# Two quads of attention heads share 32 PSUM rows, and are copied out, turned back and divided per pair

## The chip, the cores and the metric

The kernel runs on one core of one Trainium2 chip. The metric is the device time of one execution in microseconds (us); lower is better. Engines: PE is TensorE (matrix products and transposes; PEld are its weight loads), DVE is VectorE, ACT is ScalarE, POOL is GpSimd, SP only issues DMAs here.

## The reference

Eight sublayers are applied in turn to x (16 batches of 128 tokens, 128 features), each as x = x + tanh(gate) * f(layernorm(x)). The context is 16 x 128 x 128. Cut to what matters:

```
x += tanh(g_xattn[0]) * L0_xattn(ln(x), ctx)    # 0: linear causal attention
x += tanh(g_ffn[0])   * L0_ffn(ln(x))           # 1: 8 experts
x += tanh(g_xattn[1]) * L1_xattn(ln(x), ctx)    # 2: one-head attention
x += tanh(g_ffn[1])   * L1_ffn(ln(x))           # 3: 16 experts and a shared one
x += tanh(g_xattn[2]) * L2_xattn(ln(x), ctx, ctx, mask)  # 4: 16 heads of width 8
x += tanh(g_ffn[2])   * L2_ffn(ln(x))           # 5: 64 slots with a GRU step
x += tanh(g_xattn[3]) * L3_xattn(ln(x), ctx, ctx)        # 6: 16 heads; 8 of them on every 2nd token
x += tanh(g_ffn[3])   * L3_ffn(ln(x))           # 7: 32 experts and a shared one
```

In 4 and 6, for each head: attn = softmax(q k^T / sqrt(8)), out = attn v, the heads' outputs side by side, then times Wo. In 6 heads 8 to 15 use every second query, key and value, and their output is interpolated back to 128 tokens.

## The kernel before

The 16 batches are four groups of four. All data stays on the chip between sublayers. Sublayer 0 comes first, then a stream of expert work for 1 and 3 (with 2 riding on it), then a stretch `heads_*` for 4 and 6 (with 5 riding on it), then a second expert stream for 7.

The change is in the `heads_*` stretch, whose order is written out by hand. It has 8 cycles c: cycles 0 to 3 are the four groups of sublayer 4, cycles 4 to 7 those of sublayer 6. A cycle has 16 steps t, a step n = 16c + t is one unit: four heads (a quad) of one batch. Quad a is t // 4, the batch is t % 4. In cycles 4 to 7 quads 2 and 3 are the half-width ("coarse") heads. All engines walk the same n, each in its own queue, kept apart by semaphores. At step n TensorE does

- `score(n)`, L1517 and L1518: the mask (cycles 0 to 3) and the logits of the unit's four heads, into one of two banks SC;
- `shift(n-1)`, L1524: subtracts each row's maximum, which VectorE took (L1818);
- other work that has a fixed step: the next group's normalised rows (L1569), its queries and keys (L1339), its values (L1366, L1369, L1373), the last group's heads turned (L1448) and projected (L1460), results (L1579), and the slots' sublayer (`slots_pe`, L1895 to L1937);
- `turn(n-2)`, L1537: four transposes of the exponentials, which ScalarE made (L1685); ScalarE then copies them to SBUF (L1695);
- `weigh(n-3)`, L1556: the four heads' values times the turned exponentials. Each head's values are a block of 32 columns: 8 values, a one, and zeros. The product so has 32 rows per head in a bank PV: 8 of output, one of the softmax's sum, 23 of zeros;
- the turn back, `back_pe`, L1406, at some steps.

A quad's four units fill one bank PV. Then `os_act` (L1415) copies the bank to SBUF (`os`, at steps 2, 6, 10 and 14 in ScalarE's queue, behind that step's L1685 and L1695), `back_pe` (L1406) transposes it into the bank Y with four transposes (two for a coarse quad), and `divided_dve` takes the reciprocal of the sums (L1423) and multiplies (L1426). The turns back of a cycle's quads stand at its steps 10 and 12 and at steps 0 and 4 of the next cycle, the divisions one step later.

ScalarE at step 7 also copies the last group's turned heads (L1455), which TensorE's key product L1339 at step 8 waits for, since both use bank T. At step 10 it copies the next group's rows (L280), for the query product L1339 at step 11. VectorE's L1984, L1986 and L1988 at step 0 prepare the slots' state for TensorE's L1895 at step 1. GpSimd spreads the keys over four heads (L1758). The values are copied to their blocks by L1388 (sublayer 4) and L1390 and L1393 (sublayer 6), which TensorE's turn back at step 4 waits for.

Of the kernel before, what the change touches and what calls it, by code (L numbers as in the profile page):

```python
# [137 lines left out]
def build(nc, small_d, const_d, constb_d, x_d, ctx_d, mask_d, moe_d, out_d, wrow_d):  # L138
    with ExitStack() as ctx:
# [347 lines left out]
        def setup_dve(dve, st):  # L487
# [58 lines left out]
            st.add(v.memset(vh[0][:, :, DK], 1.0))  # L546
            for k in range(2):
                st.add(v.memset(vc[0][k * HALF:(k + 1) * HALF, :, k * VW + DK], 1.0))
# [400 lines left out]
        def stream_pe(pe, run):  # L949
# [34 lines left out]
            for n in range(end + LAG - (REST if run is STREAMS[0] else 0)):  # L984
                if n < end:
# [21 lines left out]
                    if (p, n) == (7, 0):  # L1007
                        back_pe(pe, 6, QUADS * NG - 1)
# [221 lines left out]
        def stream_dve(dve, st, run):  # L1230
# [8 lines left out]
            for n, (G, i) in enumerate(run.chunks):  # L1239
# [68 lines left out]
        rden = sb("rden", [P, GB * HEAD_TILES])  # L1308
# [21 lines left out]

        def back_at(q):

            return GB * q + (10 if q % QUADS == 0 else 8)
# [43 lines left out]
        def values_dve(dve, p, g):  # L1377
# [7 lines left out]
            fine = vh[g % 2][:].rearrange("p (j n) d -> p j n d", j=GB)  # L1385
            of = values_bank(p, g)
            if p == 4:
                ins = v.tensor_copy(fine[:, :, :, 0:DK], of[:].rearrange("p (j n d) -> p j n d", j=GB, d=DK))  # L1388
            else:
                v.tensor_copy(fine[:, :, 0:HEADS // 2, 0:DK],  # L1390
                              of[:, 0:2 * P].rearrange("p (j n d) -> p j n d", j=GB, d=DK))
                for k in range(2):
                    ins = v.tensor_copy(  # L1393
                        vc[g % 2][k * HALF:(k + 1) * HALF, :, k * VW:k * VW + DK],
                        of[0:HALF, 2 * P:4 * P].rearrange("p (n k d) -> p n k d", k=2, d=DK)[:, :, k, :])
            ins.then_inc(sem("heads_v_ready"), 1)
# [12 lines left out]
        def os_act(act, p, q):
            _, e, eq, eu = runs(p)  # L1410
            w = GB * width(p, q % QUADS)
            act.wait_ge(sem("heads_pv_mm"), eu + GB * (q + 1))
            if eq + q > 0:
                act.wait_ge(sem("heads_ob_mm"), eq + q)
            nc.scalar.copy(os[:, 0:w], PV[q % 2][:, 0:w]).then_inc(sem("heads_os_ready"), 1)  # L1415

        def divided_dve(dve, st, p, q):
            _, e, eq, _ = runs(p)
            a, v = q % QUADS, nc.vector
            n = GB * width(p, a) // 32  # L1420
            back = Y[:, 0:n * 32].rearrange("p (n d) -> p n d", d=32)
            dve.wait_ge(sem("heads_ob_mm"), eq + q + 1)
            st.add(v.reciprocal(rden[:, 0:n], back[:, :, DK]))  # L1423
            st.settle()
            dst = oc[:, :, 4 * (a - 2):4 * (a - 1), :] if coarse(p, a) else osb[:, :, 4 * a:4 * a + 4, :]
            v.tensor_tensor(dst, back[:, :, 0:DK].rearrange("p (x i) d -> p x i d", i=HEAD_TILES),  # L1426
                            rden[:, 0:n].rearrange("p (x i) -> p x i", i=HEAD_TILES).unsqueeze(3)
                            .to_broadcast([P, n // 4, 4, DK]), ALU.mult).then_inc(sem("heads_osb_ready"), 1)

        def upsample_pe(pe, g):  # L1430
            _, e, eq, _ = runs(6)
            pe.wait_ge(sem("heads_osb_ready"), eq + QUADS * (g + 1))
# [11 lines left out]
        def heads_turned_pe(pe, p, g):  # L1444
            _, e, eq, _ = runs(p)
            pe.wait_ge(sem("heads_osb_ready"), eq + QUADS * (g + 1))
# [51 lines left out]
        def heads_pe(pe):  # L1498
# [41 lines left out]
            def weigh(u):  # L1540
# [3 lines left out]
                w, q = width(p, a), u // GB  # L1544
# [3 lines left out]
                if j == 0 and q >= 2:  # L1548
                    pe.wait_ge(sem("heads_os_ready"), q - 1)
                heads = P // w  # L1550
                for i in range(0, HEAD_TILES, heads):
                    if coarse(p, a):
                        val = vc[g % 2][:, j * (HEADS // 4) + 2 * (a - 2) + i // 2, :]
                    else:
                        val = vh[g % 2][:, j * HEADS + 4 * a + i, :]
                    ins = mm(PV[a % 2][VW * i:VW * (i + heads), j * w:(j + 1) * w], val,  # L1556
                             pt[u % 2][:, i // heads * w:(i // heads + 1) * w], start=True, stop=True)
# [24 lines left out]
            for n in range(ALL + 3):  # L1582
# [5 lines left out]
                if c < CYCLES:  # L1588
# [37 lines left out]
                    if t == at["value"] and c + 1 < CYCLES:  # L1626
# [4 lines left out]
                        else:  # L1631
                            pe.wait_ge(sem("heads_osb_ready"), QUADS * (c - 1) + 3)
# [21 lines left out]
        def heads_act(act):  # L1654
            for n in range(ALL + 3):
# [139 lines left out]
        def heads_dve(dve, st):  # L1795
# [475 lines left out]
```

## Time and profile before

| | |
|---|---|
| median of 3 runs | 845.33 us (843.93 to 845.87) |
| the profiled execution | 845.92 us |
| its span, first to last instruction | 844.1 us |
| TensorE busy | 817.3 us, 97% |
| VectorE, ScalarE, GpSimd busy | 480.2, 424.4, 447.4 us |
| TensorE's granted clock, mean | 0.993 |
| L1406, the turn back | 112 transposes |
| L1415, the bank's copy | 32 |
| L1423 and L1426, the division | 32 each |

Busy time is the time in which at least one instruction of the engine is under way. Matmuls overlap, so one row's duration is more than what it adds; the distance between starts tells that.

### The profile page before, as it was taken

How to read it: one execution, taken by the hardware profiler on the slowest of the kernel's cores; microseconds unless marked ns; L12 is line 12 of the kernel's file. 1: busy time of each engine (PE TensorE's matmuls, PEld its weight loads, DVE VectorE, ACT ScalarE, POOL GpSimd, SP SyncE). 2: the span in 40 equal slices, each digit the busy share in tenths (PEclk: the TensorE clock that was granted, in tenths of full speed). 3: DMA queues.
4: the chain of work that ended last, by engine and by line, in shares of the span. 5: the costliest groups of instructions: out<-in, count | busy, mean ns of one | idle time of the engine just before them, and what ended most of it. 6: DMA issues, size and time to landing. Idle time of an engine off the chain costs nothing.

```text
span 844.1 us, 13575 instructions
## 1 busy us (share of the span) xinstructions
PE 817.3 (97%) x4427; PEld 557.7 (66%) x4427; DVE 480.2 (57%) x1411; ACT 424.4 (50%) x778; POOL 447.4 (53%) x429
## 2 busy tenths in 40 slices
PE   4999999999999999999999999999999999999998
PEld 4876676777667666665766666656566576666664
DVE  6766636393846555335556757576756746545332
ACT  1434555656555343334667676756556562424231
POOL 5375656466654546376454444353555357565453
PEclk9799999999999999999999999999999999999999
DMA  9213030214422141441334131312123051424251
GB/s 313 86 49 101 1 101 1 99 65 158 133 82 87 56 145 53 142 124 35 80 94 113 42 98 36 104 42 61 48 54 86 23 156 62 155 62 149 73 153 47
DMA packets 44870, 75.29 MB, mean 89 GB/s; under 512 B 8992, under 2 KB 9632, under 8 KB 44672
## 3 DMA queue, kind: packets, MB, share of 16 engines
q1 hardware_dynamic: 44656, 74.42, 29.9%
q8 instruction: 36, 0.59, 0.3%
q14 instruction: 34, 0.28, 0.1%
q10 hardware_dynamic: 144, 0.01, 0.0%
HBM read 56.11 MB, written 1.51 MB: 68 GB/s over the span
## 4 chain that ended last, share of the span: by engine, by line
PE 89%; DVE 5%; ACT 3%; issue 2%; DMA 1%; SPq 0%; ACTq 0%; DVEq 0%
PE Y L945 21%; PE B L872 11%; PE B L870 11%; PE B L871 11%; PE B L1537 5%; PE B L1556 4%; PE B L1518 3%; PE B L1524 3%; PE B L1517 2%; PE T L1339 2%; PE Y L1406 2%; PE T L962 1%; DVE mxh L1818 1%; PE Y L1460 1%; DMA CT<-in_ctx_t 1%
## 5 line engine op out<-in xcount | busy, mean ns | idle before, releaser
L1213 POOL TENSOR_TENSOR shared<-shared,bcs 128x512 f32<-128x512 f32 x192 | 248.0, 1297 | 213.5 <-DVE shared L1249 189.6
L1249 DVE TENSOR_TENSOR shared<-shared,B 128x512 f32<-128x512 f32 x204 | 139.7, 686 | 221.6 <-PE B L872 184.1
L1085 ACT ACTIVATE shared<-B 128x512 f32<-128x512 f32 x204 | 121.8, 599 | 252.2 <-PE B L872 251.4
L945 PE MATMUL Y<-shared,down_lo 128*128 128x512 f32 x408 | 207.5, 594 | 0.0
L1758 POOL TENSOR_TENSOR shared_r<-shared_r,const 128x512 fp32r<-128x512 f32 (+1 forms) x128 | 115.7, 936 | 82.8 <-PE B L1518 52.2
L1818 DVE TENSOR_REDUCE mxh<-B 128x4 fp32r<-128x512 f32 (+1 forms) x128 | 78.9, 618 | 83.0 <-PE B L1518 82.2
L1685 ACT ACTIVATE shared<-B 128x512 f32<-128x512 f32 (+1 forms) x128 | 69.7, 544 | 49.9 <-PE B L1524 48.3
L1695 ACT COPY shared<-B 128x512 f32<-128x512 f32 (+1 forms) x128 | 64.7, 506 | 57.2 <-PE B L1537 57.1
L945 PEld LDWEIGHTS Y<-shared,down_lo 128*128 128x128 f32 x408 | 72.5, 190 | 21.4 <-issue 9.5
L870 PE MATMUL B<-shared_r,gate_hi 128*128 128x512 f32 x102 | 81.0, 794 | 0.0
L870 PE MATMUL B<-x_lo_r,gate_hi 128*128 128x512 f32 x102 | 75.6, 741 | 0.0
L1537 PE MATMUL B<-const,shared 128*128 128x128 f32 x448 | 71.5, 276 | 0.0
L1518 PE MATMUL B<-shared_r 128*128 128x512 f32 (+1 forms) x128 | 66.9, 523 | 2.0 <-ACT shared L1685 2.0
L1537 PEld LDWEIGHTS B<-const,shared 128*128 128x128 f32 x448 | 53.3, 141 | 22.6 <-issue 13.5
L1524 PE MATMUL B<-mxh,minus_r 128*128 128x512 f32 (+1 forms) x128 | 47.6, 372 | 2.4 <-DVE mxh L1818 2.1
L1556 PE MATMUL B<-shared,vh 128*32 128x128 f32 x768 | 40.9, 285 | 0.0
L871 PE MATMUL B<-x_hi_r,gate_hi 128*128 128x512 f32 x102 | 40.5, 397 | 0.0
L872 PE MATMUL B<-shared_r,up_lo_r 128*128 128x512 f32 x102 | 40.5, 397 | 0.0
L872 PE MATMUL B<-x_hi_r,up_lo_r 128*128 128x512 f32 x102 | 40.4, 396 | 0.0
L872 PE MATMUL B<-x_hi_r,gate_lo_r 128*128 128x512 f32 x102 | 40.3, 395 | 0.0
L871 PE MATMUL B<-x_hi_r,up_hi 128*128 128x512 f32 x102 | 40.3, 395 | 0.0
L870 PE MATMUL B<-x_lo_r,up_hi 128*128 128x512 f32 x102 | 40.2, 394 | 0.0
(317 smaller groups left out, 1426.8 us busy)
## 6 DMA issues: line engine op xcount, KB each, us to landing
bcs<-wrow SPq DMA_DIRECT2D x96, 256.0 KB, 3.8
shared_r<-shared_r SPq DMA_DIRECT2D x256, 64.0 KB, 2.0
bcs<-wrow SPq DMA_DIRECT2D x128, 128.0 KB, 3.1
gate_lo<-in_moe SPq DMA_DIRECT2D x9, 256.0 KB, 5.3
up_lo<-in_moe SPq DMA_DIRECT2D x9, 256.0 KB, 6.3
down_lo<-in_moe SPq DMA_DIRECT2D x9, 256.0 KB, 3.6
small<-in_small SPq DMA_DIRECT2D x1, 1372.5 KB, 10.6
X<-in_x SPq DMA_DIRECT2D x4, 256.0 KB, 5.1
```

Of the source, the lines that this page charges most:

```text
L870: nc.tensor.matmul(out, w_hi[w][:, cols], lo, start=start, stop=False)
L871: nc.tensor.matmul(out, w_hi[w][:, cols], hi, start=False, stop=False)
L872: return nc.tensor.matmul(out, w_lo[w][:, cols], hi, start=False, stop=stop)
L945: nc.tensor.matmul(Y[:], w_raw[2][:, at:at + P], hid[(n0 + c) % HIDDEN], start=(i == 0), stop=(i == m["NC"] - 1))\
L1085: nc.scalar.activation(sg[(n0 + n) % ACTIVE], B[n % GATES][:], ACT.Silu).then_inc(sem("sg_ready"), 1)
L1213: gp.tensor_tensor(hid[(n0 + n) % HIDDEN], hid[(n0 + n) % HIDDEN], bcs[(PLACE.k0[p] + r // m["PER"]) % BROADCAST], ALU.mult)\
L1249: nc.vector.tensor_tensor(hid[(n0 + n) % HIDDEN], sg[(n0 + n) % ACTIVE], up[:], ALU.mult)\
L1518: mm(out, qh[a][:, cols], k_each[a % 2][:, :, cols], start=(p == 6), stop=True)\
L1537: ins = nc.tensor.transpose(PT[:, c], es[u % 2][:, c], ident)
L1556: ins = mm(PV[a % 2][VW * i:VW * (i + heads), j * w:(j + 1) * w], val, pt[u % 2][:, i // heads * w:(i // heads + 1) * w], start=True, stop ...
L1758: ins = nc.gpsimd.tensor_tensor(k_each[a % 2][:, i, cols], kh[a % 2][:, cols].bitcast(F32), K("rowmask")[:, i:i + 1].to_broadcast([P, TG * ...
L1818: v.tensor_reduce(mxh[n % 2][0:w, :], SC[n % 2][0:w, 0:4 * w].rearrange("p (i k) -> p i k", i=4), AX.X, ALU.max).then_inc(sem("max_ready"), 1)
```

## The change

Two quads, a pair, share the 32 PSUM rows of each of four blocks. The values of head pairs are laid out so that the even quad's values and its one stand in columns 0 to 8 of the block and the odd quad's in columns 16 to 24, zeros elsewhere; the eight units of a pair are added into one bank PV. Only the pair's first unit has the start flag. Copy, turn back and division are then done once per pair, over the same bank width; the division takes 32 sums and 256 values (16 and 128 for the coarse pair). `PAIRS` is 2, `PU` is 8. The turns back stand at step 12 and at step 4 of the next cycle, the copies at steps 10 and 2. The columns of Wq, Wk and their biases are reordered on the host, so that a pair's heads alternate between its two quads. The description also names the slots' logits in PSUM and moved tiles of GpSimd; of these the diff has no line.

```diff
+        rden = sb("rden", [P, GB * HEADS // 2])
+        def fine_at(h):
+            return vh[h][:].rearrange("p (m b) (y z) -> p m (b y) z", b=2, z=2 * DK)[:, :, 0:4:3, :]
+        def coarse_at(h, k):
+            return vc[h][k * HALF:(k + 1) * HALF].rearrange("p (m b) (y z) -> p m (b y) z", b=2, z=2 * DK)\
+                [:, :, 2 * k:2 * k + 6:5, :]
+        PAIRS, PU = QUADS // 2, 2 * GB
         def back_at(q):
-            return GB * q + (10 if q % QUADS == 0 else 8)
+            return PU * q + 12
...
# values_dve
-                v.tensor_copy(fine[:, :, 0:HEADS // 2, 0:DK],
-                              of[:, 0:2 * P].rearrange("p (j n d) -> p j n d", j=GB, d=DK))
+                for b in range(2):
+                    v.tensor_copy(half[:, :, 0:HEADS // 4, b, :], half_of[:, :, :, b, :])
...
# back_pe
-            for x in range(GB * width(p, q % QUADS) // P):
+            for x in range(GB * width(p, 2 * (q % PAIRS)) // P):
                 ins = nc.tensor.transpose(Y[:, x * P:(x + 1) * P], os[:, x * P:(x + 1) * P], ident)
...
# os_act
-            act.wait_ge(sem("heads_pv_mm"), eu + GB * (q + 1))
+            act.wait_ge(sem("heads_pv_mm"), eu + PU * (q + 1))
...
# divided_dve
-            n = GB * width(p, a) // 32
-            back = Y[:, 0:n * 32].rearrange("p (n d) -> p n d", d=32)
+            n = GB * width(p, 2 * pair) // (2 * DK)
+            back = Y[:, 0:n * 2 * DK].rearrange("p (n d) -> p n d", d=2 * DK)
             st.add(v.reciprocal(rden[:, 0:n], back[:, :, DK]))
             st.settle()
-            v.tensor_tensor(dst, back[:, :, 0:DK].rearrange("p (x i) d -> p x i d", i=HEAD_TILES),
+            v.tensor_tensor(dst, back[:, :, 0:DK].rearrange("p (x i) d -> p x i d", i=H8),
...
# weigh
-                w, q = width(p, a), u // GB
+                w, q = width(p, a), u // PU
-                    ins = mm(PV[a % 2][VW * i:VW * (i + heads), j * w:(j + 1) * w], val,
-                             pt[u % 2][:, i // heads * w:(i // heads + 1) * w], start=True, stop=True)
+                    ins = mm(PV[q % 2][VW * i:VW * (i + heads), j * w:(j + 1) * w], val,
+                             pt[u % 2][:, i // heads * w:(i // heads + 1) * w], start=(u % PU == 0), stop=True,
+                             skip_group_check=True)
...
# heads_pe, at the end of a step
-                for q in (n // GB - 2, n // GB - 3):
-                    if 0 <= q < ALL // GB and back_at(q) == n:
-                        if q % QUADS == 2 and 3 <= c <= 2 + NG:
-                            pe.wait_ge(*slots_done("act", "at", c - 3))
-                        elif q % QUADS == 3 and c + 1 < CYCLES:
-                            pe.wait_ge(sem("heads_v_ready"), c + 2)
-                        back_pe(pe, group(q // QUADS)[0], q % (QUADS * NG))
+                q = (n - back_at(0)) // PU
+                if 0 <= q < ALL // PU and back_at(q) == n:
+                    if q % PAIRS == 1 and c + 1 < CYCLES:
+                        pe.wait_ge(sem("heads_v_ready"), c + 2)
+                    back_pe(pe, group(q // PAIRS)[0], q % (PAIRS * NG))
...
# heads_act
-                q = (n - 6) // GB
-                if n % GB == 2 and 0 <= q < ALL // GB:
-                    os_act(act, group(q // QUADS)[0], q % (QUADS * NG))
+                q = (n - PU - 2) // PU
+                if n % PU == 2 and 0 <= q < ALL // PU:
+                    os_act(act, group(q // PAIRS)[0], q % (PAIRS * NG))
...
# slots_pe, steps 2 and 14
-                pe.wait_ge(sem("heads_osb_ready"), QUADS * (c - 1) + 3)
+                pe.wait_ge(sem("heads_osb_ready"), PAIRS * (c - 1) + 1)
-                pe.wait_ge(sem("heads_osb_ready"), QUADS * c + 2)
+                pe.wait_ge(sem("heads_osb_ready"), PAIRS * c + 1)
...
# layout, on the host
+    by_quad = np.arange(HEADS * DK).reshape(HEADS // 8, HEAD_TILES, 2, DK).transpose(0, 2, 1, 3).reshape(-1)
+    for name in ("Wq4", "Wk4", "Wq6", "Wk6"):
+        small[name] = small[name][:, by_quad]
+    for name in ("bq4", "bk4", "bq6", "bk6"):
+        small[name] = small[name][by_quad]
```

## Rows read from the trace of the kernel before

**Rows 1.** Page, part 1: engine, busy us (share), instructions.
```profile
PE 817.3 (97%) x4427; PEld 557.7 (66%) x4427; DVE 480.2 (57%) x1411; ACT 424.4 (50%) x778; POOL 447.4 (53%) x429
```

**Rows 2.** Timeline, TensorE, cycle 2: start, us, engine, line, operation, out<-in, count.
```profile
448.15 0.38 PE L1524 MATMUL B<-mxh,minus_r 128*128 128x512 f32 x1
...
449.25 0.66 PE L1406 MATMUL Y<-const,shared 128*128 128x128 f32 x4
...
450.19 0.38 PE L1524 MATMUL B<-mxh,minus_r 128*128 128x512 f32 x1
...
451.75 0.38 PE L1524 MATMUL B<-mxh,minus_r 128*128 128x512 f32 x1
```

**Rows 3.** Timeline, TensorE, cycle 7, steps 4 and 10.
```profile
653.75 0.44 PE L1406 MATMUL Y<-const,shared 128*128 128x128 f32 x2
653.94 0.48 PE L1518 MATMUL B<-shared_r 128*128 128x512 f32 x1
...
666.05 0.66 PE L1406 MATMUL Y<-const,shared 128*128 128x128 f32 x4
666.47 0.47 PE L1518 MATMUL B<-shared_r 128*64 128x256 f32 x1
```

**Rows 4.** Waits, 381 to 681 us: who waited <- for whom: us, times, longest.
```profile
PEld B L1524 <- DVE mxh L1818: 6.8, 14, 1.3
...
PEld T L1339 <- ACT shared L1455: 4.6, 6, 1.1
```

**Rows 5.** Timeline, ScalarE, cycle 1, steps 6 and 7.
```profile
430.09 0.59 ACT L1415 COPY shared<-B 128x512 f32<-128x512 f32 x1
430.57 0.60 ACT L1455 COPY shared<-T 128x512 f32<-128x512 f32 x1
```

**Rows 6.** Timeline, ScalarE and weight loads, steps 10 and 11, cycles 1 and 5.
```profile
437.83 0.59 ACT L280 COPY xhat_t<-T 128x512 f32<-128x512 f32 x1
438.54 0.40 PEld L1339 LDWEIGHTS T<-xhat_t,small 128*128 128x128 f32 x2
...
600.83 0.59 ACT L280 COPY xhat_t<-T 128x512 f32<-128x512 f32 x1
601.97 0.30 PEld L1339 LDWEIGHTS T<-xhat_t,small 128*128 128x128 f32 x2
```

**Rows 7.** Timeline, VectorE and TensorE, cycle 4, steps 0 and 1.
```profile
532.90 0.42 DVE L1988 TENSOR_TENSOR x_lo<-x_lo,B 128x256 f32<-128x256 f32 x1
533.55 0.65 PE L1895 MATMUL B<-wvo,x_lo 128*64 128x128 f32 x4
```

**Rows 8.** Chain of waits, cycle 5, steps 0 and 1: start, us, what.
```profile
573.35 0.43 DVE x_lo L1988
...
573.82 1.09 PE B L1895 x8
```

**Rows 9.** Timeline, TensorE, cycle 7, step 8; in brackets idle before, and its releaser.
```profile
662.27 0.42 PE L1518 MATMUL B<-shared_r 128*64 128x256 f32 x1 [0.40 <-ACT shared L1685]
```

**Rows 10.** Groups by form, VectorE, 381 to 681 us: busy us, mean ns, idle before.
```profile
L2032 DVE RECIPROCAL shared<-B 128x256 f32<-128x256 f32 x4 | 7.0, 1757 | 0.1
L1426 DVE TENSOR_TENSOR shared<-Y,rden 128x128 f32<-128x128 f32 x24 | 7.0, 291 | 0.8
L1423 DVE RECIPROCAL rden<-Y 128x16 f32<-128x16 f32 x24 | 5.9, 248 | 0.2
...
L1393 DVE COPY vc<-Y 64x128 f32<-64x128 f32 x8 | 2.2, 278 | 0.1
...
L2046 DVE TENSOR_TENSOR t<-t,B 128x256 f32<-128x256 f32 x4 | 1.7, 420 | 0.1
...
L684 DVE TENSOR_TENSOR vals<-s,gm 128x128 f32<-128x128 f32 x1 | 1.0, 973 | 0.0
```

**Rows 11.** Chain of waits, cycle 6, steps 13 to 15.
```profile
642.57 0.27 DVE rden L1423
...
645.61 0.32 PE B L1524
```

More of the change, by code:

```diff
@@ L545, in setup_dve @@
             st.settle()
-            st.add(v.memset(vh[0][:, :, DK], 1.0))
+            st.add(v.memset(fine_at(0)[:, :, :, DK], 1.0))
             for k in range(2):
-                st.add(v.memset(vc[0][k * HALF:(k + 1) * HALF, :, k * VW + DK], 1.0))
+                st.add(v.memset(coarse_at(0, k)[:, :, :, DK], 1.0))
             st.settle()
@@ L1409, in os_act @@
         def os_act(act, p, q):
-            _, e, eq, eu = runs(p)
-            w = GB * width(p, q % QUADS)
-            act.wait_ge(sem("heads_pv_mm"), eu + GB * (q + 1))
-            if eq + q > 0:
-                act.wait_ge(sem("heads_ob_mm"), eq + q)
+            _, e, _, eu = runs(p)
+            w = GB * width(p, 2 * (q % PAIRS))
+            act.wait_ge(sem("heads_pv_mm"), eu + PU * (q + 1))
+            if PAIRS * e + q > 0:
+                act.wait_ge(sem("heads_ob_mm"), PAIRS * e + q)
             nc.scalar.copy(os[:, 0:w], PV[q % 2][:, 0:w]).then_inc(sem("heads_os_ready"), 1)
         def divided_dve(dve, st, p, q):
-            _, e, eq, _ = runs(p)
-            a, v = q % QUADS, nc.vector
-            n = GB * width(p, a) // 32
-            back = Y[:, 0:n * 32].rearrange("p (n d) -> p n d", d=32)
-            dve.wait_ge(sem("heads_ob_mm"), eq + q + 1)
+            _, e, _, _ = runs(p)
+            v, pair = nc.vector, q % PAIRS
+            H8 = HEADS // 2
+            n = GB * width(p, 2 * pair) // (2 * DK)
+            back = Y[:, 0:n * 2 * DK].rearrange("p (n d) -> p n d", d=2 * DK)
+            dve.wait_ge(sem("heads_ob_mm"), PAIRS * e + q + 1)
             st.add(v.reciprocal(rden[:, 0:n], back[:, :, DK]))
             st.settle()
-            dst = oc[:, :, 4 * (a - 2):4 * (a - 1), :] if coarse(p, a) else osb[:, :, 4 * a:4 * a + 4, :]
-            v.tensor_tensor(dst, back[:, :, 0:DK].rearrange("p (x i) d -> p x i d", i=HEAD_TILES),
-                            rden[:, 0:n].rearrange("p (x i) -> p x i", i=HEAD_TILES).unsqueeze(3)
-                            .to_broadcast([P, n // 4, 4, DK]), ALU.mult).then_inc(sem("heads_osb_ready"), 1)
+            dst = oc[:] if coarse(p, 2 * pair) else osb[:, :, H8 * pair:H8 * (pair + 1), :]
+            v.tensor_tensor(dst, back[:, :, 0:DK].rearrange("p (x i) d -> p x i d", i=H8),
+                            rden[:, 0:n].rearrange("p (x i) -> p x i", i=H8).unsqueeze(3)
+                            .to_broadcast([P, n // H8, H8, DK]), ALU.mult).then_inc(sem("heads_osb_ready"), 1)
         def upsample_pe(pe, g):
-            _, e, eq, _ = runs(6)
-            pe.wait_ge(sem("heads_osb_ready"), eq + QUADS * (g + 1))
+            _, e, _, _ = runs(6)
+            pe.wait_ge(sem("heads_osb_ready"), PAIRS * (e + g + 1))
             for y in range(2):
@@ L1444, in heads_turned_pe @@
         def heads_turned_pe(pe, p, g):
-            _, e, eq, _ = runs(p)
-            pe.wait_ge(sem("heads_osb_ready"), eq + QUADS * (g + 1))
+            _, e, _, _ = runs(p)
+            pe.wait_ge(sem("heads_osb_ready"), PAIRS * (e + g + 1))
             for j in range(GB):
@@ L1547, in weigh @@
                     pe.wait_ge(sem("heads_v_ready"), c + 1)
-                if j == 0 and q >= 2:
+                if u % PU == 0 and q >= 2:
                     pe.wait_ge(sem("heads_os_ready"), q - 1)
@@ L1805, in divide @@
             def divide(n):
-                for q in (n // GB - 2, n // GB - 3):
-                    if 0 <= q < ALL // GB and back_at(q) + 1 == n:
-                        divided_dve(dve, st, group(q // QUADS)[0], q % (QUADS * NG))
+                q = (n - back_at(0) - 1) // PU
+                if 0 <= q < ALL // PU and back_at(q) + 1 == n:
+                    divided_dve(dve, st, group(q // PAIRS)[0], q % (PAIRS * NG))
             pieces = route_dve(dve, st, 7)
```

36 lines of the change are left out of this document (18 added, 18 removed).

## The prediction

> **What bounds the kernel now.** I read the page first, then TensorE's timeline over the attention stretch (381 to 676 us, all that the change touches after the setup), then the waits there, then the chain of waits, then what VectorE and ScalarE do where the chain leaves TensorE. The page has TensorE busy 97% of the span and the other three about half [rows 1]. Busy alone proves little, since matmul rows overlap; the timeline is better. In it a plain step, from one L1524 to the next, takes 1.56 us (450.19 to 451.75), and the step before it, with a turn back (L1406) in it, takes 2.04 [rows 2]: four transposes hold the queue 0.48. In cycles 4 to 7 four hold it 0.42 and two 0.19 [rows 3]. So what is taken out of such a step shortens it, as long as nobody else is then late.
>
> Waits are few but decide the rest. TensorE's weight loads wait 4.6 us in six places for ScalarE's copy L1455 (step 8 of cycles 1 to 6), and 6.8 us in fourteen for VectorE's maximum [rows 4]. In each of the six places L1455 stands right behind a copy L1415 in ScalarE's queue [rows 5], and the chain of waits runs through both.
>
> **A rule against it.** Page 1 of the profile gives weight loads 66% of the span [rows 1]. The Trainium skill, page "Perfetto Trace Analysis", section "Identifying the Most-Contended Engine", says that matmul busy time doesn't measure TensorE's headroom and that the share of its weight loads does; by that rule a third of its time would be spare. Rival B is what this would mean here.
>
> **TensorE's transposes.** Before, each group has four turns back, at steps 10 and 12 of its cycle and at 0 and 4 of the next; after, two, at 12 and 4, as wide as those that stood there. Gone are the batches at step 10 of cycles 0 to 7 (four transposes each) and those at step 0 of the cycles that follow (four each for the groups of cycles 0 to 3, two each for those of 4 to 7, the last one at loop step 128): 56 of 112 transposes. Their price is what they hold, not how long their rows last (0.66 us for four), which overlaps their neighbours: 8 batches x 0.48 + 4 x 0.42 + 4 x 0.19 = 3.84 + 1.68 + 0.76 = **6.3 us** [rows 2, 3]. The skill's page "TensorE: Matmul & The Clock Gate", section "PE-mode transpose", names about 275 ns for one in a kernel. The trace doesn't bear that out as a price: four of them span 0.66 us and hold 0.48 [rows 2], where four times 0.275 would be 1.1; by it the sum would have 15.4 us in place of 6.3.
>
> **What of it is given back.** Step 11 begins with a load for L1339, which needs ScalarE's copy L280. In cycle 1 this copy ends at 437.83 + 0.59 = 438.42 and the load starts at 438.54 [rows 6]; without the turn back the load could start 0.48 sooner, and gets 0.07 (0.05 go from a copy's end to its follower). The copy stays where it is: it follows transposes of L1537 that come before the turn back. Cycles 1 to 3 are alike: 3 x 0.41 = 1.2 us. In cycles 4 to 6 the copy ahead of L280 is short, L280 ends at 601.42 and the load starts at 601.97 [rows 6], so 0.5 is free and all but 0.05 is kept. Cycles 0 and 7 have no such copy there. From step 0 to 1 of cycles 3 to 6 TensorE needs L1988 from VectorE. In cycle 4 that ends at 533.32 and L1895 starts at 533.55 [rows 7]: of 0.48, 0.18 stays. In cycle 5 it ends at 573.78 and L1895 starts at 573.82 [rows 8]: nothing is kept of 0.19, nor in cycle 6. Cycle 3 has more room than 4 and loses 0.09. 0.09 + 0.30 + 0.19 + 0.19 = 0.8. Together **2.05 us given back**; 4.2 stay.
>
> **ScalarE's copies.** L1415 runs 16 times, not 32; those at steps 6 and 14 go. An engine at 50% gains nothing from that by itself, and those at step 14 are hidden. At step 6 L1415 puts L1455 off by 430.57 - 430.09 = 0.48 us [rows 5], and TensorE waits more than that for L1455 (4.6 / 6 = 0.77). Cycles 1, 2, 5 and 6 gain 0.48 each; cycle 3 gains 0.40 and cycle 4 only 0.10, as VectorE's maximum, which comes nearly as late and gets later (next part), is then the last. Cycle 7 has L1415 ahead of the exponential for which TensorE idles 0.40 [rows 9]: 0.40. Sum **2.8 us**. Bounds: 0, if another wait takes over at once, and 7 x 0.48 = 3.4.
>
> **VectorE's larger divisions.** 32 reciprocals and multiplies become 16 pairs of twice the size. No reciprocal of 32 columns is in the trace; 16 take 248 ns and 256 take 1757, a line through which gives 0.35 us for 32 [rows 10]. The multiply over 256 columns lies between the present one over 128 (0.29) and twice the slowest over 128 in the trace (L684, 0.97, so 1.9); ordinary ones over 256 take 0.42 [rows 10], the nearest row, and I take that. A full pair costs 0.80 in place of 0.57, so +0.24; the pair of half-width heads at step 5 +0.12. At steps 1 and 11 a division goes away that nobody waited for, but in cycle 7 it frees VectorE so that L893 keeps up. At steps 5 and 13 the addition lies ahead of the next maximum. Mostly VectorE waits there for scores and it is free. It is on the path at step 13 of cycle 6, where the chain has reciprocal, multiply and normalisation without a gap up to L1524 at 645.61, for which TensorE idled [rows 11]; at step 13 of cycle 4, ahead of the L1988 of [rows 8]; and at step 5 of cycle 1: 3 x 0.24. At step 5 of cycles 6 and 7: 2 x 0.12. For half-width groups the values' copy over 256 columns becomes two over 128 at 0.28 each [rows 10]: between 0 and 0.28 more, I take 0.14; in cycles 3 to 5 that hides behind two table loads of ScalarE, in cycle 6 it shows. Sum **1.1 us lost**. Bounds: 0 and 16 x 0.24 = 3.8.
>
> **At nothing:** the weights' columns, reordered on the host; the products (L1556), whose count and shape stay, with other columns and start flags; the waits at steps 0 to 2 and 14 on an earlier or equal division; ScalarE's copies at steps 2 and 10, which stay in place; GpSimd and the DMAs, of which no instruction moves, and for whose tiles TensorE has no wait in this stretch that matters. The words of the change also name the slots' logits in PSUM and GpSimd's tiles; the diff has no line on either, and the logits are in a bank already.
>
> **Sum.** 6.28 - 2.05 + 2.82 - 1.12 = 5.9 us. The profiled execution took 845.92 us (span 844.1, and 1.8 around it): 840.0. The median of the runs shown is 845.33, 0.6 lower, so 839.4; I say 839.5.
>
> **Rivals.**
> A, *the freed slots turn into waits*: a step's exponential ends shortly before the matmul that needs it, so ScalarE may pace the steps as soon as they shrink, and the wait at step 8 pass to another. For it: fourteen waits for the maximum [rows 4]. Against it: the plain steps of 1.56, with the same ScalarE and VectorE work. Kept are only step 10 of cycles 0 and 7, step 0 of 1 and 2 and the last two batches, 0.48 + 0.42 + 2 x 0.48 + 2 x 0.19 = 2.2, less 1.1: 844.2. Chance 0.10.
> B, *TensorE has time to spare*: its holds would be refilled from its slack, the 6.3 and the 2.8 worth nothing: 845.3. Against it the two step lengths in [rows 2]. It is what the page on trace analysis would lead to. Chance 0.05.
> C, *slower, the doubled division holds up the maximum*: the multiply reads PSUM with gaps and spreads one factor over 8 columns; at L684's rate a pair would take 0.35 + 1.9 against 0.57, 1.7 more, 1.3 past VectorE's idle time (an estimate), at 12 of 16 places: 15.6 us, against the 7.05 that the rest brings: 853.9. It decides from 0.44 us on the path per division. Against it: the 24 multiplies of this form take 0.29 on the mean [rows 10]. Chance 0.06.
> D, *more than forecast*: VectorE swallows its divisions and L280 starts sooner: 6.3 + 3.4 less 1.5: 837.1. Chance 0.09.
> The forecast has 0.70. That the change doesn't do what it says needs no case: its instructions and waits are explicit.
>
> **From cases to numbers.** The same means within 0.2% (1.7 us), about what a measurement of this kernel can tell. The forecast and D are faster; A is same in 7 of 10 cases; B is same; C slower. Faster 0.83, same 0.11, slower 0.06. Range: 6.3 + 3.4 with 1.0 lost gives 836.6; upward it takes in the forecast with half of each gain gone and stops short of A: 843.4.
>
> **What would show it.** 56 transposes in L1406; in cycles 0 and 1 steps 10 and 0 shorter by 0.4 to 0.5; a new wait of 0.3 to 0.4 for L280 at step 11 of cycles 1 to 3; L1339's wait for L1455 down from 4.6 to about 2; 16 copies L1415; reciprocals near 0.35 and multiplies near 0.42; the attention stretch shorter by 5.9 and the expert streams around it unchanged. I am wrong if step 0 of cycles 1 and 2 keeps its length, if the multiply is above 0.6, or if the streams move.

## The result and the profile after

| | before | after |
|---|---|---|
| median, us | 846.41 (842.57 to 849.64, 10 runs) | 840.84 (838.66 to 842.71, 10 runs) |
| profiled execution, its span | 845.92, 844.1 | 840.37, 838.6 |
| ratio, 95% interval | | 0.9927 [0.9909, 0.9946] |

The change saves 5.6 us of 846. Forecast were 839.5 us and a saving of 5.9. The page's part 1 of the kernel after, against [rows 1] (engine, busy us and share, instructions):

```profile
PE 812.8 (97%) x4371; PEld 552.5 (66%) x4371; DVE 476.2 (57%) x1383; ACT 417.8 (50%) x762; POOL 446.2 (53%) x429
```

56 matmul instructions are gone, 16 of ScalarE's and, on balance, 28 of VectorE's (16 reciprocals and 16 multiplies fewer, 4 copies for the half-width values more). The shares say nothing of where the time went. The timeline does: TensorE at the starts of steps 0, 1 and 2 of cycle 2, the place of [rows 2].

```profile
445.57 0.38 PE L1539 MATMUL B<-mxh,minus_r 128*128 128x512 f32 x1
...
447.13 0.38 PE L1539 MATMUL B<-mxh,minus_r 128*128 128x512 f32 x1
...
448.69 0.38 PE L1539 MATMUL B<-mxh,minus_r 128*128 128x512 f32 x1
```

Both steps take 1.56 us; step 0, which held the turn back, took 2.04. Waits in the attention stretch, 376 to 676 us, against [rows 4] (who waited <- for whom: us, times, longest):

```profile
PEld B L1539 <- DVE mxh L1832: 9.6, 16, 1.7
...
PE B L1539 <- DVE mxh L1832: 4.1, 7, 1.4
...
PEld T L1351 <- ACT xhat_t L280: 1.4, 3, 0.5
PEld T L1351 <- ACT shared L1470: 1.1, 2, 0.6
```

The wait for the copy of the turned heads (L1470, before L1455) fell from 4.6 us to 1.1; a new one for L280 came in three cycles; the one for the maximum grew from 6.8 to 9.6. ScalarE in cycle 1 against [rows 5]: nothing stands ahead of L1470 any more but the step's own copy.

```profile
427.69 0.59 ACT L1709 COPY shared<-B 128x512 f32<-128x512 f32 x1 [0.28 <-PE B L1552]
428.17 0.59 ACT L1470 COPY shared<-T 128x512 f32<-128x512 f32 x1
```

VectorE's division by form, 376 to 676 us, against [rows 10] (busy us, mean ns | idle before):

```profile
L1441 DVE TENSOR_TENSOR shared<-Y,rden 128x256 f32<-128x256 f32 x12 | 5.1, 425 | 0.4
L1438 DVE RECIPROCAL rden<-Y 128x32 f32<-128x32 f32 x12 | 4.2, 352 | 0.2
```

0.42 and 0.35 us, as taken from neighbouring rows.

**Step by step.** A step runs from one L1524 (L1539) to the next. The difference after - before, us, wherever it is over 0.04:

```
steps 10 and 0                  -5.81  (-0.48 each in cycles 0 to 3; 4: -0.39, -0.19; then -0.45, -0.18)
steps 11 and 1, given back      +1.46  (L280: 3 x 0.30; L2001: 0.10, 0.08, 0.20, 0.17)
step 8                          -3.81  (-0.48 -0.69 -0.66 -0.40 -0.62 -0.49 -0.47)
steps 6 and 7, division         +1.30  (+0.25 +0.20 +0.25 +0.23 +0.13 +0.12 +0.12)
step 14, division               +0.37  (cycles 4 and 5)
step 4, values                  +0.07  (cycle 6)
cycle 6, step 15                +0.98
cycle 7, steps 1 and 2          +1.12
cycle 7, steps 11 and 12        -0.04  (+0.23, -0.27)
first to last L1524             -4.34
```

Before the stretch the profiled execution after is 1.2 us ahead with the same instructions. The first 31 us cost both the same in granted clock (5.1 us of full clock), so it isn't the clock; what it is, no run shows. From the last L1524 to the end the two agree within 0.01, so the last turn back that went, at loop step 128, gave nothing.

**What was not foreseen** are the two lines on step 15 of cycle 6 and on steps 1 and 2 of cycle 7. VectorE and GpSimd there, and TensorE:

```profile
636.99 2.56 DVE L1815 TENSOR_SCALAR xhat<-X,mv,rstd 128x128 f32<-128x128 f32 x4
...
637.39 4.07 POOL L1772 TENSOR_TENSOR shared_r<-shared_r,const 128x512 fp32r<-128x512 f32 x4 [0.91 <-PE B L1533]
...
639.48 1.00 DVE L1832 TENSOR_REDUCE mxh<-B 64x4 fp32r<-64x256 f32 x2
...
639.94 0.32 PE L1539 MATMUL B<-mxh,minus_r 64*64 64x256 f32 x1 [1.35 <-DVE mxh L1832]
...
641.57 1.06 PE L1585 MATMUL T<-const,xhat 128*128 128x128 f32 x4
```

Four tiles of the normalisation take 2.56 us while GpSimd spreads keys; the maximum behind them is late, TensorE idles 1.35 us, and soon after four transposes last 1.06. The windows of that stretch (us; busy and count of PE, PEld, DVE, ACT, POOL; granted clock; DMA share, GB/s) say why:

```profile
638.00:641.00 3.00, 1.65 (x13) 0.89 (x10) 2.48 (x4) 0.80 (x3) 3.00 (x4) 1.00 0.43 105
641.00:644.00 3.00, 3.00 (x14) 2.22 (x14) 0.69 (x1) 1.47 (x4) 0.47 (x1) 0.53 0.40 97
644.00:647.00 3.00, 3.00 (x23) 2.48 (x22) 1.98 (x3) 2.17 (x4) 1.04 (x2) 0.90 0.29 66
```

The granted clock fell to 0.5, the level of 1.2 GHz; over the windows of 1 us this drop takes away 1.7 us of full clock. It made the steps 1.1 us longer.

### The profile page after: what moved, and what is told of

Same layout as the page of the kernel before. It is cut to its first block, busy times and chain, and to the rows that moved or that the text cites. A ratio compares the mean times of both kernels' runs of the same rounds, so it can differ in the third digit from the quotient of the medians.

```text
span 838.6 us, 13371 instructions
## 1 busy us (share of the span) xinstructions
PE 812.8 (97%) x4371; PEld 552.5 (66%) x4371; DVE 476.2 (57%) x1383; ACT 417.8 (50%) x762; POOL 446.2 (53%) x429
## 4 chain that ended last, share of the span: by engine, by line
PE 87%; DVE 7%; ACT 2%; issue 2%; DMA 1%; SPq 0%; ACTq 0%; DVEq 0%
PE Y L945 21%; PE B L870 11%; PE B L872 11%; PE B L871 11%; PE B L1552 5%; PE B L1571 3%; PE B L1533 3%; PE B L1539 3%; PE B L1532 2%; PE T L1351 2%; DVE mxh L1832 2%; PE T L962 1%; DVE xhat L1815 1%; DMA CT<-in_ctx_t 1%; PE Y L1475 1%
## 5 line engine op out<-in xcount | busy, mean ns | idle before, releaser
L1772 POOL TENSOR_TENSOR shared_r<-shared_r,const 128x512 fp32r<-128x512 f32 (+1 forms) x128 | 115.6, 933 | 79.5 <-PE B L1533 37.4
L1539 PE MATMUL B<-mxh,minus_r 128*128 128x512 f32 (+1 forms) x128 | 48.3, 377 | 4.4 <-DVE mxh L1832 4.1
```

What stands on the lines that cost most here:

```text
L1539: mm(SC[u % 2][0:w, 0:4 * w].rearrange("p (i k) -> p i k", i=HEAD_TILES), minus_r[0:w, 0:w], mxh[u % 2][0:w, :].unsqueeze(2).to_broadcast( ...
L1772: ins = nc.gpsimd.tensor_tensor(k_each[a % 2][:, i, cols], kh[a % 2][:, cols].bitcast(F32), K("rowmask")[:, i:i + 1].to_broadcast([P, TG * ...
```

## The experiments

**How they are compared.** Executions of one kernel differ by up to 9 us, and their mean granted clock differs with them: a line through the 203 runs of all kernels, with an offset for each, has 0.67 us for each 0.001 of clock (plus or minus 0.03), and leaves 0.63 us. So the table gives beside the median the time that this line gives each kernel at a clock of 0.994, with its 95% interval. The ratio is to the runs of the kernel before from the same batch; their medians are 844.5 (e1, e2, e4, e6), 846.5 (e3, e8, e9, e10) and 846.0 (e7, e11, e12), and at 0.994 the three batches agree within 0.2 us.

| kernel | runs | median (range) | ratio to before | mean clock | at 0.994 |
|---|---|---|---|---|---|
| before | 79 | 846.0 (842.5 to 851.6) | | 0.9922 | 845.1 ± 0.2 |
| after | 10 | 840.8 (838.7 to 842.7) | 0.9927 [0.9909, 0.9946] | 0.9924 | 839.7 ± 0.4 |
| e1_turns_again | 12 | 846.5 (843.3 to 850.1) | 0.9998 [0.9975, 1.0021] | 0.9902 | 843.8 ± 0.4 |
| e2_copies_again | 12 | 845.3 (842.1 to 847.4) | 0.9993 [0.9971, 1.0015] | 0.9906 | 842.7 ± 0.4 |
| e6_before_copy_late | 12 | 845.2 (842.1 to 846.9) | 0.9995 [0.9975, 1.0015] | 0.9922 | 843.8 ± 0.4 |
| e3_multiply_twice | 12 | 848.9 (846.8 to 850.5) | 1.0023 [1.0003, 1.0043] | 0.9880 | 844.8 ± 0.4 |
| e4_keys_after_norm | 6 | 837.7 (836.0 to 838.8) | 0.9895 [0.9869, 0.9922] | 0.9948 | 838.0 ± 0.5 |
| e7_before_keys_wait | 12 | 845.6 (843.3 to 848.4) | 0.9983 [0.9962, 1.0003] | 0.9928 | 844.8 ± 0.4 |
| e9_filled_last_idle | 6 | 840.0 (837.5 to 843.1) | 0.9916 [0.9884, 0.9947] | 0.9937 | 839.7 ± 0.5 |
| e8_filled_idle | 6 | 836.6 (836.0 to 837.6) | 0.9877 [0.9850, 0.9904] | 0.9953 | 837.6 ± 0.5 |
| e11_before_filled | 12 | 844.9 (844.4 to 848.1) | 0.9985 [0.9966, 1.0004] | 0.9942 | 845.5 ± 0.4 |
| e12_before_both | 12 | 845.6 (843.8 to 847.1) | 0.9978 [0.9959, 0.9997] | 0.9941 | 845.5 ± 0.4 |
| e10_query_late | 12 | 842.2 (840.0 to 846.5) | 0.9949 [0.9926, 0.9973] | 0.9928 | 841.9 ± 0.4 |

### TensorE's part: e1_turns_again

```diff
+                if t in (0, 10) and n >= 10:
+                    # waits as before, then
+                    for x in range(2 if t == 0 and again >= NG else 4):
+                        nc.tensor.transpose(Y[:, x * P:(x + 1) * P], ident, ident)
```

> The changed kernel with as many transposes put back where the turns back of the other quads stood (steps 10 and 0: four each, two each at step 0 after the groups of sublayer 6). They turn a constant into the bank Y and nobody reads them, so this adds TensorE's part alone: no copy of ScalarE and no division. Theory (the holds are real time on TensorE): steps 10 and 0 longer by 0.48, 0.42 or 0.19, 6.0 us in all, of which 1.5 comes back at steps 11 and 1, where L280 and L2001 are waited for less: +4.5 us on 840.8, 845.3. Rival A (waits took the freed time): +1.1 to +2.2 us, 842 to 843. Rival B (TensorE has time to spare): 840.8, unchanged.

Measured: 4.1 us more at an equal clock. Steps 10 longer by 0.45 to 0.48, steps 0 by 0.48 to 0.50, 0.38 and 0.17; steps 11 shorter by 0.30, steps 1 by 0.07 to 0.17. Cycle 4's step 10 alone differs: +0.46, where the removal had given 0.19 (e2 finds the rest). Step 0 of cycle 7 (+0.98) and steps 4 to 8 of cycle 2 (+3.1) lie beside clock drops and tell nothing. The holds are real, rivals A and B fall. The median is 5.7 above, because this kernel's clock is also lower (below).

### ScalarE's part: e2_copies_again and e6_before_copy_late

```diff
+                if n % PU == 6 and n > PU:
+                    q, wide = n // PU - 1, GB * width(group(c)[0], 0 if t == 6 else 2)
+                    nc.scalar.copy(spare[:, 0:wide], PV[q % 2][:, 0:wide])
```

> The changed kernel with ScalarE's copies at steps 6 and 14 put back, as large as before, from the bank that rests there into a tile that nobody reads (the one at step 6 of cycle 0 is left out). TensorE and VectorE keep their instructions. Theory (the copy at step 6 stood ahead of L1470, for which TensorE waits at step 8): TensorE's loads wait about 4 us for L1470 in place of 1.1, step 8 is longer by about 0.4 in cycles 1 to 7, +2.5 to +2.8 us: 843.5. Rival (the gain at step 8 came from the missing transposes, or another wait takes over): 840.8 to 841.3. The copies at step 14 cost nothing by either.

Measured: 3.0 more at an equal clock. ScalarE in cycle 1, and the waits of 376 to 676 us:

```profile
425.93 0.59 ACT L1715 COPY shared<-B 128x512 f32<-128x512 f32 x1
426.40 0.60 ACT L1471 COPY shared<-T 128x512 f32<-128x512 f32 x1
```

```profile
PEld T L1352 <- ACT shared L1471: 4.3, 6, 1.1
```

Steps 7 and 8 of cycles 1 to 7 are longer by 0.48, 0.49, 0.42, 0.28, 0.49, 0.49 and 0.48, 3.1 in all, and cycle 4 gets 0.28 back at step 10. Beside that only steps around clock drops (cycle 2, steps 5 and 6, and five of cycle 7) and one of 0.12 moved: the copies at step 14 cost nothing. So the copies are worth 3.1 less 0.28, or 2.9, and nothing at all in cycle 4: what step 8 gains there comes back at step 10. That is why step 10 of cycle 4 gave 0.19 when its transposes went, and costs 0.46 when they come back.

The same from the other side, with nothing removed:

```diff
# before.py: the copy of step 6 goes to the end of step 7
+                late = n % NU == 7
+                q = (n - 6 - late) // GB
```

> The kernel before with one thing moved: the bank's copy L1415 of step 6 is issued at the end of step 7, behind L1455. Nothing is removed. Theory (the order in ScalarE's queue was worth 2.8 us of the 5.9 forecast): L1455 runs 0.48 sooner, TensorE's wait for it falls from 4.6 to about 2, step 8 is shorter by 0.4 to 0.5 in most cycles: 2.3 to 2.8 us less than the kernel before, 843.8. Rival (that wait was due to TensorE's own lateness or passes to the maximum): less than 0.5 us.

Measured: 1.3 less at an equal clock, half of what I said. Step 8 did get shorter, by 0.40 to 0.50 in cycles 1 to 7 (3.3 in all) and the wait fell as expected:

```profile
PEld T L1339 <- ACT shared L1455: 1.7, 5, 0.6
```

But step 9 of cycle 0 got longer by 0.40, and step 10 of cycles 1 to 6 by 0.19 to 0.39, 1.5 in all. The moved copy now stands ahead of the key's, L1349. In cycle 1 that starts at 433.62 where it started at 433.31 before:

```profile
433.14 0.59 ACT L1415 COPY shared<-B 128x512 f32<-128x512 f32 x1
433.62 0.70 ACT L1349 ACTIVATE shared_r<-T,small 128x512 fp32r<-128x512 f32 x1
```

In cycle 0 the exponential L1685 stands behind L1349, and TensorE idles 0.33 us for it. In cycle 1 VectorE's half of the key (L1355) starts no sooner than before, the normalisation stands right behind it, and TensorE's L1569 at step 10 starts 0.12 behind the end of the normalisation (436.13):

```profile
434.36 0.75 DVE L1355 SCALAR_TENSOR_TENSOR shared_r<-T,small,shared_r 128x512 fp32r<-128x512 f32 x1
435.02 1.11 DVE L1802 TENSOR_SCALAR xhat<-X,mv,rstd 128x128 f32<-128x128 f32 x4
436.25 0.42 PEld L1569 LDWEIGHTS T<-const,xhat 128*128 128x128 f32 x4 [0.49 <-issue]
```

The kernel before has the same three at 434.34, 435.00 and 436.21 and an idle time of 0.31. In all six cycles the idle time before L1569's loads grows by what step 10 does (0.19, 0.19, 0.19, 0.38, 0.27 and 0.28): TensorE comes there sooner and waits for a chain of ScalarE and VectorE that doesn't. The removal is worth more than the reordering: the copy has to stand somewhere, and each place has someone behind it.

### VectorE's part: e3_multiply_twice

```diff
+            st.add(v.tensor_tensor(dst, ... the same multiply ...))
+            st.settle()
```

> The changed kernel with the division's multiply (L1441) issued twice, the first time behind the reciprocal and waited for: one more operation of 0.42 us over 256 columns (0.29 over 128 in cycles 4 to 7 at step 5) on VectorE at 16 places. Theory (VectorE's larger division is felt where a step's maximum stands behind it and TensorE has no slack: step 5 of all cycles from 1 on, step 13 of cycles 4 to 6, not at step 13 of cycles 0 to 3): 4 x 0.42 + 3 x 0.29 + 3 x 0.42 = 3.8 us more. Rival C of the prediction (every doubled division holds up the maximum): 16 places, above 5.5 us. Rival (VectorE at half load swallows it): 0. At a granted clock of 0.994 the changed kernel takes 839.75 us, so 843.6, 845.3 or 839.8.

Measured: 5.1 more at an equal clock, above the 3.8 of the theory and close to the rival's 5.5. The added operation (L1441; L1445 is the other) takes

```profile
L1441 DVE TENSOR_TENSOR shared<-Y,rden 128x256 f32<-128x256 f32 x12 | 5.1, 424 | 0.4
...
L1445 DVE TENSOR_TENSOR shared<-Y,rden 128x256 f32<-128x256 f32 x12 | 5.1, 424 | 0.4
```

and shows almost whole in the steps: 0.45 behind step 5 in cycles 1, 3 and 4, 0.32 in 5 to 7; 0.45, 0.45, 0.41 behind step 13 in cycles 4 to 6; and 0.28 to 0.33 behind step 13 in cycles 1 to 3, which I had thought free (0.13 and 0.16 come back a step later in cycles 2 and 3; 0.1 to 0.2 more appears at step 0 of cycle 2 and step 1 of cycles 3 and 4). In cycle 2 a clock drop covers step 5. Free are only step 13 of cycles 0 and 7 and the last division, in the next stream. These steps add up to 4.6 us without cycle 2's step 5. VectorE is busy 57% of the span and idles before most maxima, but what stands directly ahead of a maximum delays it.

Not all of the added time is the multiply's own. Step 15 of cycle 6 is longer by 1.56 than in the kernel after, because the unforeseen slow normalisation gets worse: VectorE comes to it later still, in the same moment as GpSimd to its keys (643.22), all four tiles last 1.07, and TensorE idles 2.93 us for the maximum:

```profile
643.27 4.06 DVE L1819 TENSOR_SCALAR xhat<-X,mv,rstd 128x128 f32<-128x128 f32 x4
...
647.72 0.47 PE L1543 MATMUL B<-mxh,minus_r 64*64 64x256 f32 x1 [2.93 <-DVE mxh L1836]
```

With it the steps give some 6.2 us, more than the 5.1 at an equal clock. The line is a rough measure here: all of this kernel's clocks are low (0.986 to 0.990; the median is 8.1 above that of the kernel after), and in the profile one drop begins within those 2.93 us, where it holds up no work. What stays is that 3.8 was too little for the exposed multiplies.

### The missed 2.1 us: e4_keys_after_norm, e7_before_keys_wait, e9_filled_last_idle

```diff
                 if c + 1 < CYCLES:
+                    # only in cycle 6
+                    pool.wait_ge(sem("xhat_ready"), S4 + CYCLES + 1)
                     one_head_pool(pool, *group(c + 1), 1)
```

> The changed kernel with one wait more on GpSimd: in cycle 6 it starts the keys of cycle 7's second quad (L1772, 4.07 us, from 637.39) only when VectorE's normalisation L1815 is done. Theory of the missed 2.2 us (two engines in each other's way: L1815 takes 2.56 us for four tiles while L1772 runs, 1.11 elsewhere): L1815 takes 1.1, the maximum behind it is no longer late, TensorE's idle time of 1.35 at 639.94 goes and so does the stretch at half clock behind it: step 15 of cycle 6 and step 1 of cycle 7 shorter by 2.2 together, 838.4. Those keys are needed at step 4 of cycle 7 and come in time. Rival (L1815 is slow for another reason, DMA traffic or the larger division ahead of it): L1815 stays at 2.5 and the time at 840.8.

Measured: median 837.7. Step 15 of cycle 6 is shorter by 1.42, step 1 of cycle 7 by 1.27, all others by 0.00 to 0.02 (step 2 gives 0.14 back). VectorE in that kernel:

```profile
636.78 1.10 DVE L1817 TENSOR_SCALAR xhat<-X,mv,rstd 128x128 f32<-128x128 f32 x4
637.80 0.41 DVE L1834 TENSOR_REDUCE mxh<-B 64x4 fp32r<-64x256 f32 x1
```

The conflict is shown: the same four tiles take 1.10 us with GpSimd still and 2.56 with it at work (1.82 in the kernel before, 4.06 in e3: none, two, one and all four of the tiles are long). The rows of the four tiles, after and then before (ns min/median/max):

```profile
L1815 DVE TENSOR_SCALAR xhat<-X,mv,rstd x4: 329/695/1071, 637.0 to 638.5; 128x128 f32<-128x128 f32 x4
```

```profile
L1801 DVE TENSOR_SCALAR xhat<-X,mv,rstd x4: 329/330/1053, 643.4 to 644.2; 128x128 f32<-128x128 f32 x4
```

After, two of the four are long, before one; a long one lasts as long as a tile of GpSimd's (4.07 / 4). The Trainium skill, page "SBUF — State Buffer", section "Who interferes with whom", says that VectorE and GpSimd share one pair of ports, that a tensor_scalar can enter the modes that use it, and that whoever issues first has the pair for its whole instruction while the other is blocked. Tile lengths equal to GpSimd's agree with it; that it is the ports and nothing else, no run here separates.

> The kernel before with the one wait of e4_keys_after_norm (in cycle 6 GpSimd starts the keys of cycle 7's second quad only behind VectorE's normalisation). Theory (the conflict was there before, but only the end of L1801 met it: 1.82 us in place of 1.10, and TensorE idled 0.37): L1801 takes 1.1, 0.4 us less at an equal granted clock (844.7 at 0.994 against 845.1). So of the 1.8 that the same wait gave in the changed kernel some 1.4 were the change's own loss. Rival (the conflict cost the same before): 1.8 less, 843.3.

Measured: only step 15 of cycle 6 changed, by -0.43; the time at an equal clock by 0.3. So the conflict was there before and cost 0.43; the change moved VectorE's normalisation from 0.64 us ahead of GpSimd's keys (L1801 at 643.40, L1758 at 644.04) to 0.40 (L1815 at 636.99, L1772 at 637.39). So two tiles met it and not one, and 0.98 of the 1.42 are the change's own.

```diff
+                if n == (CYCLES - 1) * NU:
+                    pe.wait_ge(sem("x_updated"), S4 + CYCLES - 2)
+                    for x in range(10):
+                        nc.tensor.transpose(T[:, 0:P], ident, ident)
```

> The changed kernel (VectorE's slow normalisation stays) with 10 transposes of a constant into bank T ahead of the L1539 of cycle 7, step 0, where TensorE idles 1.35 us. It tells the idle time from the half clock behind it. Theory: the maximum is as late as before, so the 1.35 are merely filled and nothing is gained there; the stretch at half clock at 641 to 645 doesn't come, and step 1 of cycle 7 is shorter by 1.2: 839.6 in such an execution, and up to 1 us off the median of 840.8. Rival (the half clock has nothing to do with the idle time): still there, 840.8.

Measured: in the profile the idle time is filled and the same stretch keeps its clock:

```profile
642.25 1.25 PE L1605 MATMUL T<-const 128*128 128x128 f32 x10
643.76 0.32 PE L1539 MATMUL B<-mxh,minus_r 64*64 64x256 f32 x1 [0.26 <-DVE mxh L1836]
```

```profile
643.00:646.00 3.00, 2.74 (x22) 1.86 (x21) 2.00 (x4) 1.23 (x3) 2.29 (x3) 1.00 0.41 100
646.00:648.00 2.00, 1.63 (x15) 1.13 (x14) 1.21 (x2) 1.92 (x5) 0.00 (x0) 1.00 0.49 118
```

Step 15 is unchanged (+0.01) and steps 1 and 2 are shorter by 1.13: the two halves of the miss are an idle time and a clock drop behind it. The median is 0.8 lower, within the spread; this profile has a drop in cycle 2 instead. One profile would be thin evidence that filling keeps the clock, but the others side with it. At this place TensorE idles 1.35 us in after, e1 and e2 and 2.93 in e3, and all four have the drop; it idles 0.2 at most in e4, e7, e8 and e10, and none of them has it. In between, with 0.38 in before, e6 and e11 and 0.94 in e12, the last three have one.

### Idle time and the clock: e8_filled_idle, e11_before_filled, e12_before_both

Other profiles show the same drop elsewhere: in the kernels e1, e2, e3, e9 and e10 behind the idle time of 1.6 us at step 4 of cycle 2, which the kernels before, after, e4, e6 and e7 have as well without a drop. A drop can also come without such an idle time: e2 has a third one from 665.8 us on, and TensorE's longest idle time in the 9 us before it is 0.40. TensorE and windows of e1_turns_again there:

```profile
458.94 0.45 PE L1532 MATMUL B<-maskb,constb 128*128 128x512 bf16 x1 [1.61 <-ACT shared L1709]
```

```profile
456.00:458.00 2.00, 1.33 (x15) 0.66 (x13) 0.61 (x1) 1.97 (x3) 0.23 (x1) 1.00 0.45 111
458.00:459.00 1.00, 0.06 (x2) 0.06 (x2) 0.00 (x0) 0.99 (x3) 0.00 (x0) 1.00 0.70 139
459.00:460.00 1.00, 1.00 (x3) 0.81 (x4) 0.14 (x1) 0.36 (x1) 0.00 (x0) 0.57 0.94 350
```

Filling it:

```diff
+                if (c, t) == (2, 4):
+                    pe.wait_ge(sem("x_updated"), S4 + 1)
+                    for x in range(12):
+                        nc.tensor.transpose(T[:, 0:P], ident, ident)
```

> e4_keys_after_norm with 12 transposes of a constant into bank T, read by nobody, at step 4 of cycle 2, where TensorE otherwise idles 1.62 us for ScalarE's exponential (its two table loads around the slots' Gelu). They hold TensorE some 1.4 us of that. Theory (stretches at half clock, of 3.4 us each, begin in some executions within 2 us of such an idle time; the spread of the times is their number): none is left here, the runs' granted clock rises from a mean of 0.9948 and the median falls by 0.3 to 1 us below 837.7, with the slowest runs gone. Rival (the drops come from something else, as DMA bursts or the whole chip's load): the same clock and 837.7 or a little more. If 12 transposes are longer than the gap, step 4 gets longer by what is over.

> The kernel before with the 12 idle-time transposes of e8_filled_idle at step 4 of cycle 2 (the wait of 1.62 us is the same in both kernels). The kernel before spreads from 842.5 to 851.6 us with granted clocks from 0.986 to 0.998. Theory (part of this spread is stretches at half clock that begin at this idle time): the mean granted clock rises from 0.9926 by about 0.001, the median falls by 0.5 to 1 us, and the slowest runs are 2 to 3 us below 851.6; at an equal clock the time is the same, 845.1 at 0.994. Rival: clocks and spread unchanged.

> The kernel before with both edits, the wait on GpSimd and the filled idle time. Theory: 0.4 less at an equal clock (844.7 at 0.994), the mean granted clock 0.001 to 0.002 above 0.9926, median 844.2. Rival: as e7_before_keys_wait, with the clocks of the kernel before. It also says how far the changed kernel with the same two edits (836.56) leads when both have them: 7.5 by the theory.

Measured: e8 has the shortest median of all, 836.6, 9.4 us under the kernel before, and its slowest run is 837.6; but against e4 the gain of 1.1 is not resolved, and the mean clocks (0.9948, 0.9953) hardly differ. In e11 the mean clock rose from 0.9922 to 0.9942 and the slowest of 12 runs is 848.1 where the 79 of the kernel before reach 851.6; the median fell by 1.1, an interval that touches 1. These are the theory's numbers, but its cause isn't shown. e7, in the same batch and with nothing filled, has a slowest run of 848.4 and a mean clock of 0.9928, which 12 runs can't tell from 0.9942. And a large part of the half clock lies in the first 31 us, where no edit acts: it takes 5.1 us of full clock in before, after, e1, e3, e4, e6, e7 and e9, 3.4 in e8, e10, e11 and e12 and 1.7 in e2. One step of 1.7 there is a mean clock of 0.002, all that e11 rose by. Its profile has a drop from 643 us on, behind an idle time of 0.38 us, so filling one place doesn't end them. e12 brought nothing over e11 that can be told: in its profile VectorE's normalisation takes 1.10 us, but TensorE now waits 0.94 at that place for a query's transfer, and a drop follows. The 7.5 us by which the changed kernel with both edits should lead come out as 845.6 - 836.6 = 9.0, or 7.9 at an equal clock. That a drop often follows an idle time is supported; that filling one shortens the runs is not shown, and what decides in which execution a drop comes stays open.

### Taking the given-back time: e10_query_late

```diff
+                if t == 11 and 0 < c < CYCLES - 1:   # behind turn(n - 2)
+                    compact_pe(pe, *group(c + 1), "q")
```

> e4_keys_after_norm with the query product (L1351) of step 11 in cycles 1 to 6 issued behind the turn of that step instead of ahead of it, and ScalarE's copy of it at the end of its step 11. Theory (at step 11 of cycles 1 to 3 TensorE's load waits 0.3 for L280, which is what the removed turns back gave back): that wait goes, 3 x 0.3 = 0.9 us less, 836.8 against 837.7 (837.1 against 838.0 at a granted clock of 0.994). Rival (the wait passes to ScalarE's copy or to the result's turn at step 13, which needs VectorE's second half of the query): 0, or up to 1 us slower.

Measured: slower than e4 by 3.9 at an equal clock; the rival holds, and four times as strongly as it said. Step 11 does lose its 0.3 in cycles 1 to 3, but step 13 of cycles 1 to 6 is longer by 0.55 to 0.94, for the result's turn now waits for VectorE's half of the query (step 13 of cycle 1):

```profile
440.86 0.63 PE L1595 MATMUL T<-const,ysb 128*128 128x128 f32 x4 [0.59 <-DVE shared_r L1367]
```

## Why the prediction was right

It was right within 1.3 us (839.5 against 840.8) and in the saving (5.9 against 5.6; 5.4 ± 0.4 at an equal clock). The mechanisms of its four terms are borne out. That the sum fits so well is partly luck: too much given back (0.5) and too little loss in cycle 6 (0.7) nearly cancel. Its steps, with e1 and e2 to tell the transposes from the copies:

- **Transposes, 6.3 us.** 6.1 were forecast without the last batch, and 5.8 measured; the 0.28 that the copy takes at cycle 4's step 10 (e2) belong to the transposes, which makes 6.1. The last batch (0.19) gave nothing.
- **Given back, 2.05.** Measured 1.46. The mechanism was right in every cycle named. In cycle 1 L1351's load starts 0.42 behind its step's L1539 (436.07 and 435.65), where it started with it before; but the product now starts with the load and not 0.21 behind it as before, so the step is longer by 0.30 only. In cycle 4 step 1 took 0.08 and not 0.30: L2001 ends 1.88 us behind the L1539 of step 0, the L1988 of before 2.01 behind its L1524.
- **ScalarE's copy, 2.8.** Put back, it costs 2.9 (e2), 0.42 of it in cycle 3 and nothing in cycle 4, where 0.40 and 0.10 were forecast. The 3.8 that step 8 lost are more than the copy: 1.3 of delay had just been added at steps 6 and 7.
- **VectorE's division, 1.1 lost.** The durations were right to 0.01 us. The delay shows as 1.3 at steps 6 and 7, in all cycles from 1 to 7 and not in three, but step 8 makes part of it good, so steps 6 to 8 together gave 2.51 where the copy alone is worth 3.13 there (e2): 0.6 lost. With 0.37 at step 14 (cycles 4 and 5) and 0.07 for the values' copy that is 1.06, where 0.86 were forecast outside cycle 6. "Mostly VectorE waits there for scores and it is free" is the sentence that failed: it seemed to hold because the wait at step 8 took the delay up, and e3, without that wait, shows it nearly everywhere.
- **Cycle 6, step 13 to 15.** I had 0.24 there from the chain in [rows 11]. It cost 0.98, and 1.1 more by the clock. I read the normalisation's 1.82 us as its length; in five of the other seven places four tiles take 1.10. That row already showed the conflict.
- **Rivals.** A and B are excluded by e1, C by the 0.42 us of the multiply, though e3 shows its idea sound: with 0.42 more per division it takes 844.8 ± 0.4 at an equal clock, and the gain over 845.1 is gone. D lacked the exposure of VectorE.
- **Its arithmetic.** 1.23 and 0.77 given back make 2.00, not 2.05, and the terms of VectorE 1.10, not 1.12; the sum is 6.0 and not 5.9. The cases make 0.82 for faster and 0.12 for same. None of it matters.

In the profiled execution two things that no step spoke of nearly cancel: 1.2 us gained before the stretch, where the instructions are the same, and 1.1 lost to the clock drop.

## What to carry to other kernels

Price a removed instruction by the step length with and without it, then look at the very next wait of each neighbour: the transposes and the copies came out of such rows to 0.1 us, the waits that take their place only to 0.1 to 0.7. A step that gives time back can hide a delay ahead of it; put one thing back at a time to tell them apart. That an engine is half idle is no cover for work that stands directly ahead of the instruction another engine waits for. When an edit shifts one engine by a few tenths, look at which pairs of VectorE and GpSimd instructions it brings together, and compare a row's length with the same form elsewhere; one wait on GpSimd was worth 1.7 us at an equal clock and 3.1 in the median.

## What the hardware showed beyond that

- VectorE's 128x128 tensor_scalar takes 0.33 us (0.26 from start to start), and 1.05 to 1.07 when GpSimd is in a 128x512 tensor_tensor, which is itself 1.03 to 1.10 long.
- The granted clock can fall to half behind an idle time of TensorE of 1.35 to 1.6 us, and in e6 and e11 behind one of 0.38. Each such drop took 1.7 us of full clock, one each in e1, e3 and e10 twice that. At step 4 of cycle 2 five profiles of ten with the same idle time have one.
- The spread of a kernel's times goes with its mean granted clock, 0.67 us for 0.001, which makes differences of some 0.5 us visible with 12 runs.
